# A chunked delta rule on one core: slots reordered, key copies ahead of the norms, one key projection ahead of the states

## The chip, the cores and the metric

The kernel runs on one core of one Trainium2 chip. The metric is the device time of one execution in microseconds. A core has five engines that each run their own list of instructions in order and meet only at semaphores: TensorE (PE; its weight loads are shown as PEld), VectorE (DVE), ScalarE (ACT), GpSimd (POOL) and SyncE (SP), which here starts transfers.

## What is computed

The kernel is a chain of four attention layers and four feed-forward layers. The change touches the fourth attention layer alone, a gated delta rule with 32 heads of 64 channels on two sequences of 1024 tokens of 256 features. Cut to what matters:

```python
qkvz = x @ w_qkvz.T; ba = x @ w_ba.T                  # x: the normalised activations
q, k, v = causal_conv(q, k, v, conv_w)                # 4 taps a channel
g = -exp(A_log) * softplus(a + dt_bias); beta = sigmoid(b)
q = l2norm(q) * DK ** -0.5; k = l2norm(k)
def step(S, (q_t, k_t, v_t, g_t, b_t)):               # over the tokens
    S = S * exp(g_t)
    delta = (v_t - einsum('bhk,bhkv->bhv', k_t, S)) * b_t
    S = S + k_t[..., :, None] * delta[..., None, :]
    return S, einsum('bhk,bhkv->bhv', q_t, S)
o = o * rsqrt(mean(o * o) + EPS) * norm_weight * sigmoid(z)
return o @ w_out.T                                    # added to the residual
```

The kernel does it in chunks of 64 tokens: inside a chunk the recurrence becomes the inverse of a unit lower triangular matrix of 64 x 64 and a few products, and a state of 64 x 64 is handed from chunk to chunk, 16 chunks for a sequence.

## The kernel before

**Units.** Two heads are done together, one in partitions 0 to 63 and one in 64 to 127. A pair of heads and a batch make a unit; there are 16 pairs and 2 batches, so 32 units. `run` calls `step(t, u, f, p)` once a unit on every engine, with four units in flight: `p` (u + 2) is projected and convolved, `f` (u + 1) has its decays, key products and inverse made, `u` runs its states, and `t` (u - 1) is normalised, gated and projected out. Two steps form the body of a hardware loop.

**TensorE** gives the order. `key_side` (L2647): `turn_keys` transposes the keys of f into the PSUM banks B3 and B3+1; `decay` makes the decay exponents in A3, A3+1; `values_and_keys` (L2476) makes u's w and u parts in groups of 8 chunks, `key_products` (L2548) f's products of keys with keys and queries into A3 or B3, `key_sums` (L2664) the matrices of u's states, `decay_upto` (L2541) the decays of the queries. Then `states` (L2700): a chain over 16 chunks. `across(c)` (L2790, L2794) needs state c, which VectorE writes (L3147 for the first, L3149 for the others); `within(c + 1)` (L2768, L2776) does not. After each chunk `beside(c)` puts one piece of other work into the slot: projections `project(p, 0..5)` (L2495), `mean_square` (L2557), the gate's `project_z` (L2504), the output `project_out(t, 0..3)` (L2565, halves by `out_part`), `turn_values` (L2513, the line of both turns), and from slot 9 on the block inverse of f, in products of 32 x 32 (`inverse_y` in slot 9 to `inverse_above` in slot 14, all L2483). `hold` is a wait with an instruction of its own.

**VectorE**, one queue: `convolve` (L3010, nine a unit: kind and tap), `keys` (L3018 to L3026: the sum of squares of the keys, its reciprocal, the two scaled copies of the keys out of B3), `decayed` and `decayed_pairs` (L3040, L3046: products times decays), the sums pT (L3143), then the loop over the states q = 0 to 14 with pieces behind each: `diagonals`, `gather` (L3054, L3061: the diagonal blocks for GpSimd), `decayed_queries` (L3069), `gate` (L3080), `add` (L3087, the residual), `scatter` (L3074, the solved blocks back), `values` (L3032), `masked`, `refined`, `below`, `above` (L3092 to L3107).

**ScalarE**: the squares of the keys (L2852), the exponentials of the decays (L2868, L2874), `outputs` (L2987, L2988: o and its squares out of C3), `parts` (L2936, L2937: w and u out of D3 and C3), the matrices mT (L2950), `compacted` (L2888: three quarters of the blocks to invert), `projected` (L2841, L2842), logs and roots.

**GpSimd**: `scaled` (L2375, decays times beta), `squares` (L2412), `gated` (L2420), then `solve`: the fourth quarter of the blocks (L2384), a copy of the unit blocks (L2387) and the forward substitution, 15 pairs of a product (L2395) and a difference (L2396), each on up to 64 columns and each after the one before; `sided` (L2428, L2429) shapes the result for `scatter`; `gates` and `spread` follow.

**SyncE** loads weights by the counts of projections that TensorE has done.

## Time and profile before

| what | us |
|---|---|
| median of three runs | 4861.91 |
| lowest, highest of them | 4851.96, 4862.69 |
| the profiled execution | 4822.35 |
| its span, first to last instruction | 4820.6 |
| TensorE busy in the span | 4109.9 (85%) |
| VectorE | 2341.0 (49%) |
| ScalarE | 1668.1 (35%) |
| GpSimd | 1264.3 (26%) |

Busy time is the time in which an engine has an instruction of the program at work. The profile is one execution; a statement on an instruction's length comes from it, a statement on the time of the kernel from the runs. The delta rule's 32 steps lie between 2798 and 4594 us of the span, a good third of the kernel. In the timeline a row gives start and length in microseconds, engine, line, operation, result and operands, their form and how many; in square brackets stands how long the engine was idle before and what ended that.

### The profile page before, as it was taken

The page shows a single profiled execution, that of the slowest core. Times are in us where ns is not written, and L with a number is a line of the kernel's source. Part 1 is how long each engine was busy: PE and PEld are TensorE (multiplying, and loading weights), DVE is VectorE, ACT ScalarE, POOL GpSimd, SP SyncE.
Part 4 walks back from the last instruction along what each step waited for, and adds up shares of the span by engine and source line. Part 5 has one row for each costly group of instructions (what it writes and reads, how often), then busy time and mean ns, then how long its engine had stood idle before and what let it go on. Part 6 is the DMA issues. An engine that isn't in the chain of part 4 may idle for free. (4 is left out here: it accounts for less than half of the span.)

```text
span 4820.6 us, 107874 instructions
## 1 busy us (share of the span) xinstructions
PE 4109.9 (85%) x45061; PEld 2478.0 (51%) x45120; DVE 2341.0 (49%) x4073; ACT 1668.1 (35%) x2600; POOL 1264.3 (26%) x1755
## 2 busy tenths in 40 slices
PE   6789759999967859779899589989999889899869
PEld 3333645555534634446556355555555555555546
DVE  5942244545453251440332456666666666666541
ACT  2057122111220113231110345555555555555432
POOL 2000110000015241210000244454455554444412
PEclk9689769999978977889899789998999999889889
DMA  1000000000021510000100000000000000000000
GB/s 46 1 1 1 28 24 1 10 10 7 4 94 56 177 58 0 0 22 1 53 1 1 14 8 9 8 8 8 8 8 8 8 8 8 8 8 8 5 15 18
DMA packets 37930, 91.58 MB, mean 19 GB/s; under 512 B 6993, under 2 KB 27252, under 8 KB 33999
## 3 DMA queue, kind: packets, MB, share of 16 engines
q1 hardware_dynamic: 27150, 69.45, 4.2%
q0 software_dynamic: 6144, 11.62, 0.8%
q8 instruction: 359, 5.88, 0.5%
q10 hardware_dynamic: 4224, 4.19, 0.3%
q14 instruction: 53, 0.43, 0.0%
HBM read 69.96 MB, written 20.45 MB: 19 GB/s over the span
## 5 line engine op out<-in xcount | busy, mean ns | idle before, releaser
L2495 PE MATMUL ps<-h_normT,h_w 128*128 128x512 f32 (+1 forms) x1008 | 476.5, 582 | 76.9 <-DVE h_xx L3074 70.3
L3010 DVE SCALAR_TENSOR_TENSOR h_cv<-h_raw,h_cw,h_cv 128x1023 f32<-128x1023 f32 (+2 forms) x288 | 369.7, 1293 | 20.7 <-ACT h_cv L2842 18.7
L3149 DVE SCALAR_TENSOR_TENSOR h_st<-h_st,d_gcs,ps 128x64 f32<-128x64 f32 x448 | 123.6, 276 | 442.7 <-PE ps L2790 442.2
L2841 ACT ACTIVATE h_raw<-ps 128x512 f32<-128x512 f32 x192 | 114.1, 594 | 469.1 <-PE ps L2495 468.2
L2495 PEld LDWEIGHTS ps<-h_normT,h_w 128*128 128x128 f32 x1008 | 180.9, 211 | 170.8 <-issue 150.1
L2396 POOL TENSOR_TENSOR h_gm<-h_gm,h_tmp 128x15 f32<-128x15 f32 (+7 forms) x480 | 255.3, 532 | 37.6
L837 PE MATMUL ps<-a_probT,a_v 128*128 128x512 f32 x512 | 227.6, 603 | 0.8 <-DVE a_probT L975 0.8
L2395 POOL TENSOR_TENSOR h_tmp<-h_gm 128x15 f32<-128x15 f32 (+7 forms) x480 | 188.9, 394 | 96.5 <-DVE h_gm L3061 61.4
L1960 PE MATMUL ps<-h_normT,e_wgu 128*128 128x512 f32 (+1 forms) x448 | 204.1, 599 | 2.3 <-DMA e_wd<-in_e_wd 1.1
L2790 PEld LDWEIGHTS ps<-h_st,h_mT 64*64 64x64 f32 x1792 | 93.1, 139 | 213.7 <-issue 209.1
L2404 POOL TENSOR_TENSOR h_xT<-h_xx,d_const 32x512 f32<-32x512 f32 x64 | 66.2, 1034 | 487.6 <-DVE h_xx L3097 485.2
L1124 POOL MEMSET r_zero<- 128x2048 f32 x1 | 1.8, 1804 | 727.9 <-POOLq L54 727.9
L2565 PE MATMUL ps<-h_wo,h_o 128*128 128x256 f32 x512 | 172.7, 456 | 5.5 <-DVE h_o L3080 4.7
L407 ACT ACTIVATE a_prob<-ps 128x1024 f32<-128x1024 f32 (+1 forms) x192 | 153.8, 810 | 57.3 <-PE ps L335 19.1
L448 DVE TENSOR_REDUCE a_mx<-ps 128x2 f32<-128x1024 f32 (+2 forms) x192 | 169.2, 952 | 1.9 <-PE ps L296 1.0
L932 ACT ACTIVATE a_prob<-ps,a_nbias 128x1024 f32<-128x1024 f32 x64 | 71.3, 1113 | 284.6 <-DVE a_nbias L985 284.6
L2794 PE MATMUL ps<-h_pT,h_st 64*64 64x64 f32 x1920 | 165.4, 251 | 0.6 <-DVE h_st L3149 0.6
L837 PEld LDWEIGHTS ps<-a_probT,a_v 128*128 128x128 f32 x512 | 98.7, 194 | 124.8 <-issue 123.6
L2790 PE MATMUL ps<-h_st,h_mT 64*64 64x64 f32 x1792 | 154.8, 251 | 6.5 <-DVE h_st L3149 5.6
L148 PE MATMUL ps<-ident,h_norm 128*128 128x128 f32 x256 | 45.3, 360 | 134.7 <-DVE h_norm L127 134.7
L975 DVE COPY a_probT<-ps 128x512 f32<-128x512 f32 x128 | 82.6, 685 | 155.2 <-PE ps L887 155.2
L2548 PE MATMUL ps<-h_cv 64*64 64x128 f32 x2048 | 82.2, 293 | 77.9 <-DVE h_norm L3026 76.6
(537 smaller groups left out, 9492.1 us busy)
## 6 DMA issues: line engine op xcount, KB each, us to landing
m_wgu<-in_m_wgu SPq DMA_DIRECT2D x8, 1408.0 KB
h_w<-in_d_w SPq DMA_DIRECT2D x48, 128.0 KB, 2.2
m_wd<-in_m_wd SPq DMA_DIRECT2D x8, 704.0 KB
m_rows_in<-r_zero SPq DMA_DIRECT2D x4, 1024.0 KB, 14.1
e_xe<-m_rows_in SPq DMA_DIRECT2D x8, 512.0 KB
m_rows_out<-e_y ACTq DMA_DIRECT2D x8, 512.0 KB, 11.2
e_wgu<-in_e_wgu SPq DMA_DIRECT2D x1, 3520.0 KB
a_t_raw<-in_t_w SPq DMA_DIRECT2D x4, 768.0 KB
```

The source lines that it names most:

```text
L407: act.activation(prob[:, u % 3, :, c0:BANK], ps[:, 2 * (u % 3):2 * (u % 3) + 2, c0:BANK], ACT.Exp, scale=1.0 / float(np.sqrt(D0))).then_in ...
L448: dve.tensor_reduce(mx[:, b * NQ + qt, part, m:m + 5:4], ps[:, 2 * (n % 3):2 * (n % 3) + 2, 0:w], AX.X, ALU.max).then_inc(mx_ready, 1)
L837: last = pe.matmul(ps[:, 6 + m, :], v[:, b * NQ + kt, m * P:(m + 1) * P], probT[:, blk % 2, kt, :], start=(kt == 0), stop=(kt == NQ - 1))
L1960: last = pe.matmul(ps[0:m, 3 * (n % 2) + s, :], wgu[:, k, s, c * P:c * P + m], hT[:, k, tok], start=(k == 0), stop=(k == KC - 1))
L2395: c.link(pool.tensor_tensor(part, column, row, ALU.mult))
L2396: c.link(pool.tensor_tensor(target, target, part, ALU.subtract))
L2495: last = pe.matmul(ps[:, PROJ[m], lo:hi], w[:, kind, k, :], hT[:, k, b * S + tb * BANK + lo:b * S + tb * BANK + hi], start=(k == 0), stop= ...
L2565: last = pe.matmul(ps[:, POUT[k], j * H:(j + 1) * H], o[:, tile * P:(tile + 1) * P], wo[:], start=True, stop=True)
L2790: last = pe.matmul(ps[rows(h), D3 + c % 2, 0:HALF], mT[rows(h), c, :], st[rows(h), c, :], start=False, stop=True, tile_position=(64 * h, 6 ...
L2794: last = pe.matmul(res(h, c), st[rows(h), c, :], pT[rows(h), c, :], start=False, stop=True, tile_position=(64 * h, 64 * (1 - h)))
L3010: dve.scalar_tensor_tensor(out=d, in0=raw[:, kind, 0:S - back], scalar=tap(pr, kind, TAPS3 - 1 - back), in1=d, op0=ALU.mult, op1=ALU.add). ...
L3149: last = dve.scalar_tensor_tensor(out=st[:, q + 1, :], in0=st[:, q, :], scalar=scal(gcs, pr, b)[:, q:q + 1], in1=ps[:, D3 + q % 2, 0:HALF] ...
```

## The change

It moves work; no product is added or taken away.

- **Keys.** VectorE makes the copies with `eg` first and in two halves, before the sum of squares; ScalarE's square of the keys is in two halves, in turn with them over the two banks. The copy with `kds` comes last, and `k_ev` counts all three; `kd_d` goes.
- **Order of TensorE in `key_side`.** `key_products(f, 1)` goes behind `values_and_keys(1)`; the wait for the residual's last addition goes from the start to `decay`.
- **One projection ahead.** `project(p, 0)` leaves slot 0 and stands before the states, behind `decay_upto`. The later pieces move up a slot or more: mean square 2 -> 1, gate projection 3 -> 2 and 7 -> 6, projections 4, 5 -> 3, 4, output projections 6, 10, 12, 13 -> 5, 7, 10, and 12 and 13 by halves.
- **Copies.** ScalarE's `outputs` goes ahead of and between the squares of the keys and the decays; `compacted` goes between the two copies of mT.
- **GpSimd.** The fourth quarter (`last_quarter`) goes from behind `gated` to ahead of it.
- **VectorE.** `convolve(f, 6)` goes from before `keys` to between the two `decayed`; `diagonals` and `gather` from behind the first state copy to ahead of it; `decayed_queries`, the other convolutions, `gate` and `add` move up; `below` goes from slot 13 to slot 14; `convolve(p, 5)` goes from the end of the step to slot 12, `add(t, 3)` to the end.

```diff
-        POUT = (B3 + 1, A3, A3, B3)
+        POUT = (B3 + 1, B3 + 1, A3, A3)
...
+            def last_quarter(f, t=None):
+                n = f[0]
+                pool.wait_ge(sqa, 2 * t[0] + 2) if t else pool.wait_ge(db_d, 2 * n + 2)
+                pool.wait_ge(nt_d, 2 * n + 2)
+                pool.tensor_tensor(y[quarter(3), :, :], nT[quarter(3), :, side(3)], one(3), ALU.mult).then_inc(nc3_d, 1)
+                pool.wait_ge(nc3_d, n + 1)
...
                 if t:
                     squares(t)
+                if f:
+                    last_quarter(f, t)
+                if t:
                     gated(t)
                 if f:
-                    solve(f, t)
+                    solve(f)
...
             def key_side(t, u, f, p):
...
-                if t:
-                    hold(xa, 4 * n)
                 if f:
                     hold(ev, 6 * f[0] + 6)
                     hold(x_d, 2 * n + 2)
                     turn_keys(f)
                     hold(y4_d, 2 * n + 2)
+                    if t:
+                        hold(xa, 4 * n)
                     decay(f)
...
-                if f:
-                    hold(k_ev, f[0] + 1)
-                    key_products(f, 1)
                 if t:
                     hold(sqo_d, 2 * n)
                 values_and_keys(1)
+                if f:
+                    hold(k_ev, 3 * f[0] + 3)
+                    key_products(f, 1)
                 key_sums(0)
                 key_sums(1)
                 if f:
                     pe.wait_ge(at_d, 2 * f[0] + 1)
                     decay_upto(f)
+                if p:
+                    pe.wait_ge(at_d, 2 * f[0] + 2)
+                    project(p, 0)
...
                     if c == 0 and p:
-                        pe.wait_ge(at_d, 2 * f[0] + 2)
-                        project(p, 0)
-                    if c == 1 and p:
                         project(p, 1)
-                    if c == 2 and t:
+                    if c == 1 and t:
...
-                    if c == 3:
+                    if c == 2:
...
-                    if c == 7:
+                    if c == 6:
                         pe.wait_ge(zv, 2 * n + 1)
                         project_z(u, 1)
+                    if c == 7 and t:
+                        pe.wait_ge(xa, 4 * n + 1)
+                        project_out(t, 1)
...
                     if c == 10 and t:
                         pe.wait_ge(v_ev, f[0] + 1) if f else pe.wait_ge(lnd, 2 * t[0] + 2)
-                        project_out(t, 1)
+                        project_out(t, 2)
...
                         if f:
-                            inverse_zt(f, (lambda k: out_part(t, 2, k)) if t else None)
+                            inverse_zt(f, (lambda k: out_part(t, 3, 0) if k == 0 else None) if t else None)
...
                         if t:
-                            pe.wait_ge(ev, 6 * p[0] + 6) if p else pe.wait_ge(zv, 2 * n + 2)
-                            project_out(t, 3)
+                            out_part(t, 3, 1)
...
             def key_squares(f):
                 n = f[0]
-                act.wait_ge(trk, n + 1)
-                act.activation(flat(ksq[:]), ps[:, B3:B3 + 2, :].rearrange("p a n -> p (a n)"), ACT.Square).then_inc(ksq_d, 1)
+                for a in range(2):
+                    act.wait_ge(k_ev, 3 * n + 1) if a else act.wait_ge(trk, n + 1)
+                    act.activation(flat(ksq[:])[:, half(a)], ps[:, B3 + a, :], ACT.Square).then_inc(ksq_d, 1)
...
+                if t:
+                    outputs(t, 0)
                 if f:
                     key_squares(f)
+                if t:
+                    outputs(t, 1)
+                if f:
                     decays(f)
-                if t:
-                    outputs(t)
                 parts(0)
                 parts(1)
...
                 for g in range(2):
+                    if f and g == 1:
+                        compacted(f)
                     act.wait_ge(wk, 2 * n + g + 1)
...
-                dve.wait_ge(ksq_d, n + 1)
+                for a in (1, 0):
+                    dve.wait_ge(trk, n + 1) if a else dve.wait_ge(ksq_d, 2 * n + 1)
+                    dve.tensor_tensor(parted(vk[:, b, :, 1, :])[:, a], turned(B3)[:, a], by_parity(scal(eg, pr, b))[:, a], ALU.mult).then_inc(k_ev, 1)
+                dve.wait_ge(ksq_d, 2 * n + 2)
...
-                dve.tensor_tensor(parted(ka[b][:, :, 0, :]), turned(B3), by_parity(kds[:]), ALU.mult).then_inc(kd_d, 1)
-                dve.tensor_tensor(parted(vk[:, b, :, 1, :]), turned(B3), by_parity(scal(eg, pr, b)), ALU.mult).then_inc(k_ev, 1)
+                dve.tensor_tensor(parted(ka[b][:, :, 0, :]), turned(B3), by_parity(kds[:]), ALU.mult).then_inc(k_ev, 1)
...
                 if f:
-                    convolve(f, 6)
                     keys(f)
                     decayed(f, 0)
                     decayed_pairs(f, 0)
+                    convolve(f, 6)
                     decayed(f, 1)
                     decayed_pairs(f, 1)
...
+                if f:
+                    diagonals(f)
+                    gather(f)
                 for q in range(NC3 - 1):
...
                     if f and q == 0:
-                        diagonals(f)
-                        gather(f)
-                    if f and q == 1:
                         decayed_queries(f)
-                    if f and q in (2, 3):
-                        convolve(f, q + 5)
-                    if t and q == 5:
-                        gate(t, 0)
-                    if t and q == 7:
+                    if f and q in (1, 2):
+                        convolve(f, q + 6)
+                    if t and q in (4, 5):
+                        gate(t, q - 4)
+                    if t and q == 6:
                         add(t, 0)
+                    if t and q == 8:
+                        add(t, 1)
...
                     if t and q == 11:
-                        add(t, 1)
-                        gate(t, 1)
+                        add(t, 2)
...
-                    if f and q == 13:
+                    if f and q == 14:
                         below(f)
-                    if t and q in (13, 14):
-                        add(t, q - 11)
-                    if p and q in (4, 6, 7, 10, 12):
-                        convolve(p, (4, 6, 7, 10, 12).index(q))
+                    if p and q in (3, 5, 6, 9, 10, 12):
+                        convolve(p, (3, 5, 6, 9, 10, 12).index(q))
                 if f:
                     above(f)
-                if p:
-                    convolve(p, 5)
+                if t:
+                    add(t, 3)
```

## Rows read from the trace of the kernel before

**Rows 1.** The page: TensorE's granted clock in 40 equal slices, in tenths.

```profile
PEclk9689769999978977889899789998999999889889
```

**Rows 2.** Busy time by windows, all 29 full steps (the first line names the columns).

```profile
core 0: us, PE busy (x) PEld busy (x) DVE busy (x) ACT busy (x) POOL busy (x), PEclk, DMA share, GB/s
2858.17:4542.18 1684.01, 1517.99 (x31357) 968.97 (x31378) 1058.95 (x1596) 884.98 (x1393) 839.48 (x1277) 0.92 0.03 8
```

**Rows 3.** The same by windows, state copy to scatter: one of 29, and their sum.

```profile
3379.81:3399.76 19.95, 18.86 (x248) 9.20 (x240) 12.64 (x20) 15.72 (x24) 15.73 (x33) 1.00 0.01 2
...
sum 578.43, PE 547.17 PEld 266.94 DVE 368.76 ACT 455.89 POOL 456.00; mean PE 18.87 PEld 9.20 DVE 12.72 ACT 15.72 POOL 15.72
```

**Rows 4.** The same by windows, scatter to key squares: three of 29, and their sum.

```profile
3051.16:3070.87 19.71, 18.41 (x620) 13.33 (x621) 13.40 (x21) 6.06 (x9) 5.07 (x5) 1.00 0.02 4
...
3399.76:3422.10 22.34, 20.28 (x620) 14.30 (x622) 14.37 (x22) 6.06 (x9) 5.08 (x5) 0.92 0.01 3
...
4268.02:4293.56 25.54, 23.15 (x620) 15.94 (x622) 14.40 (x22) 6.06 (x9) 5.08 (x5) 0.80 0.02 8
...
sum 675.60, PE 626.23 PEld 438.64 DVE 403.59 ACT 175.81 POOL 147.13; mean PE 21.59 PEld 15.13 DVE 13.92 ACT 6.06 POOL 5.07
```

**Rows 5.** The same by windows, key squares to state copy: one of 29, and their sum.

```profile
3422.10:3435.46 13.36, 11.04 (x221) 8.28 (x220) 9.02 (x14) 8.72 (x16) 8.15 (x8) 1.00 0.01 2
...
sum 429.97, PE 344.58 PEld 263.39 DVE 286.60 ACT 253.28 POOL 236.34; mean PE 11.88 PEld 9.08 DVE 9.88 ACT 8.73 POOL 8.15
```

**Rows 6.** Waits in the loop: us in total, times, longest; the last from 2860 to 4467.

```profile
PE ps L2548 <- DVE h_norm L3026: 70.9, 29, 3.3
PE ps L2495 <- DVE h_xx L3074: 66.5, 29, 2.6
...
PE ps L2513 <- issue: 8.1, 12, 1.2
```

**Rows 7.** Timeline of TensorE at slot 9.

```profile
3400.96 0.67 PE L2495 MATMUL ps<-h_normT,h_w 128*128 128x256 f32 x2 [2.29 <-DVE h_xx L3074]
```

**Rows 8.** Timeline of the key stretch, all engines.

```profile
3422.10 1.02 ACT L2852 ACTIVATE h_mT<-ps 128x1024 f32<-128x1024 f32 x1 [1.82 <-PE ps L2513]
...
3423.16 1.22 DVE L3018 TENSOR_REDUCE h_ssr<-h_mT 128x16 f32<-128x1024 f32 x1 [0.26 <-ACT h_mT L2852]
3423.42 1.80 PE L2476 MATMUL ps<-h_norm,h_xT 64*64 64x128 f32 x30
...
3424.97 0.33 PE L2548 MATMUL ps<-h_cv 64*64 64x128 f32 x2
...
3425.53 1.23 DVE L3025 TENSOR_TENSOR h_ka<-ps,h_kds 128x1024 f32<-128x1024 f32 x1
...
3428.03 1.10 PE L2548 MATMUL ps<-h_cv 64*64 64x128 f32 x32 [1.82 <-DVE h_norm L3026]
...
3433.17 1.98 PE L2541 MATMUL ps<-h_gm,d_const 128*128 128x512 f32 x4
...
3433.92 1.93 ACT L2888 ACTIVATE h_y<-h_nT 32x512 f32<-32x512 f32 x3
```

**Rows 9.** Timeline of GpSimd and VectorE beside it.

```profile
3427.38 2.50 POOL L2412 TENSOR_TENSOR h_sq<-h_sq,h_qsq 128x512 f32<-128x512 f32 x2
...
3437.71 0.22 POOL L2395 TENSOR_TENSOR h_tmp<-h_gm 128x15 f32<-128x15 f32 x1 [1.80 <-DVE h_gm L3061]
...
3440.42 1.28 DVE L3010 SCALAR_TENSOR_TENSOR h_cv<-h_raw,h_cw,h_cv 128x1022 f32<-128x1022 f32 x1
3440.62 1.22 POOL L2396 TENSOR_TENSOR h_gm<-h_gm,h_tmp 128x48 f32<-128x48 f32 x1
...
3447.46 0.75 POOL L2395 TENSOR_TENSOR h_tmp<-h_gm 128x60 f32<-128x60 f32 x1
```

**Rows 10.** Timeline of slot 13.

```profile
3417.01 1.13 PE L2565 MATMUL ps<-h_wo,h_o 128*128 128x256 f32 x4
3417.12 0.70 DVE L3102 TENSOR_SCALAR h_y<-ps 32x512 f32<-32x512 f32 x1 [0.53 <-PE ps L2483]
```

More of the change, by code:

```diff
@@ L2438, in start @@
                 scaled(f)
+                last_quarter(f)
                 solve(f)
@@ L2626, in start @@
                 key_products(f, 0)
-                hold(k_ev, 1)
+                hold(k_ev, 3)
                 key_products(f, 1)
@@ L2645, in start, with key_side @@
                 inverse_above(f)
-            def key_side(t, u, f):
+            def key_side(t, u, f, p):
                 n, pr, b = u
@@ L2718, in beside @@
                         project_z(u, 0)
-                    if c in (4, 5) and p:
+                    if c in (3, 4) and p:
                         if t:
-                            pe.wait_ge(lnd, 2 * t[0] + c - 3)
+                            pe.wait_ge(lnd, 2 * t[0] + c - 2)
                         else:
                             pe.wait_ge(egx, 2 * f[0] + 2)
-                        project(p, c - 2)
-                    if c == 6 and t:
+                        project(p, c - 1)
+                    if c == 5 and t:
                         if p:
@@ L2951, in step @@
                 if f:
-                    compacted(f)
                     decays_upto(f)
```

40 lines of the change are left out of this document (18 added, 22 removed).

## Prediction, made before the changed kernel was built or run

> **What bounds the kernel now.** I read the page's slices first: the changed code fills slices 24 to 38 of 40, and there TensorE's granted clock (full is 2.4 GHz, half 1.2) never stays full for long [rows 1]. So I cut the loop into its 29 full steps with the table by windows. They last 1684.0 us, 58.07 us a step, at a mean granted clock of 0.92 [rows 2]. Each step falls into three stretches, by instructions that occur once a step: the first state copy (VectorE, L3147), the first transpose that scatters the solved blocks (VectorE, L3074) and the squares of the keys (ScalarE, L2852).
>
> State copy to scatter lasts 19.95 us in 28 of 29 steps, whatever else varies: sum 578.4 us [rows 3]. A stretch so constant follows one chain: GpSimd's forward substitution (L2395, L2396), to which nothing is given between its first and last instruction. Scatter to key squares: 19.71 us at best, 23.30 us in the mean (675.6 / 29); 27 of 29 are below clock 1.00, and the length goes with the clock: 19.71 at 1.00, 22.34 at 0.92, 25.54 at 0.80 [rows 4]. Key squares to state copy: 13.36 us in the step at 3422 (13.16 at best), 14.83 in the mean (430.0 / 29) [rows 5]; 15 of 29 are below 1.00.
>
> The table of waits names what TensorE lacks: 66.5 us before L2495 for the scatter, 70.9 us before L2548 for VectorE's copy of the keys, each once a step [rows 6]. The timeline shows the order around the first: TensorE has come to the block inverse, stands 2.29 us, and starts 1.20 us after the scatter did (3399.76) [rows 3, 7]. The second is 1.82 us in the step at 3422 [rows 8]. So neither TensorE nor another engine is full: a step is a ring, key squares -> decays -> substitution -> scatter -> inverse -> next key squares, and the clock falls behind the wait in it.
>
> **Key stretch, new order.** Zero is the start of the key squares; rows of the step at 3422 [rows 8]. The copies of the keys no longer wait for the norms: VectorE takes half the bank pair (512 columns, 0.70 us, as L3102 has it [rows 10]), ScalarE squares one half while VectorE copies the other, so the last square ends at 1.4 instead of 1.02. From the reduce's start to the scaled copy L3025 is 2.37 us (3423.16 to 3425.53), and that copy takes 1.23: k_ev reaches its third count at 5.05. Before, L3026 behind it ended at 5.8.
> TensorE: the first value-and-key group starts at 1.32, and 1.55 us later (3423.42 to 3424.97) key_products(0) wants the decays. ScalarE now has two halves of squares, one output pair and two decays ahead of that: 0.8 + 4 x 0.48 + 0.6 = 3.3 (starts of its 512-column copies lie 0.48 apart). **New wait: 0.45.** Then 1.1 (L2548) + 1.55 + 1.1 + 2 x 1.1 (L2664): 9.3. k_ev at 5.05 and the w and u copies are long there, so the waits of 1.82 and 0.39 go. Then decay_upto 1.91 (L2541, 1.98 with its last overlap) and the moved project(p, 0), again 1.91: the states start at 13.1, against 13.0 before (3433.17 + 1.91). The projection is no new work: slot 0 loses it.
> VectorE: nT(0) 4.97, its pair 5.57, then convolve(f, 6), which used to stand before the reduce. Queued behind it are nT(1), and behind that compacted, the last key-sum copy, pT(1), the diagonals, and now also the first state copy, which everybody waits for. It takes 1.28 us if it runs freely (L3010 [rows 9]). The bounds of its price are 1.28 and 1.28 + 1.25, as GpSimd is at its squares (L2412, two in 2.50) then; I take 0.6 of waiting, half of one such instruction, since it meets it midway. nT(1) ends at 8.75, compacted (L2888, 1.93) at 10.7, mT(1) 11.3, pT(1) 11.9, transpose 1.08 and gather 0.48: 13.45. GpSimd: from bep at 3.3 the 8.15 us that it is busy in this stretch [rows 5], 1.28 blocked by the convolution, and 0.6 for the copy of the unit blocks (L2387): 13.3. Behind gated, in its old place, last_quarter would hold up the transpose; where it is put, both queues end together. Substitution starts at 13.9 (bounds 13.4 and 14.9), against 15.61 before (3437.71).
>
> **Substitution.** Start of L2395 to scatter: 17.70 us (3437.71 to 3435.46 + 19.95) [rows 3, 5, 9]. The rows show what lengthens it: L2396 of 48 columns takes 1.22 us while VectorE's convolution runs, 0.3 us otherwise, and a product takes 0.75 beside gate [rows 9]. Inside it remain the decayed queries and five convolutions; gate(t, 1), so far in slot 11, joins. gate(0) costs 0.45 (0.75 - 0.30). Sum 17.70 + 0.45 = 18.15 (bounds 17.9 and 18.9); **scatter at 32.05** after the squares, against 34.78 in the mean (14.83 + 19.95) and 33.3 at best.
> The Trainium skill ("SBUF — State Buffer", section "SBUF: two separate sides") says that a VectorE instruction with two SBUF inputs and a GpSimd instruction hold one port pair as an exclusive lock, for the whole instruction. By these rows the trace agrees in kind (1.22 for 0.3), with a loss a little below the instruction's own length. By the page gate(1) would cost its whole 0.75: an estimate of 0.30 more a step, 9 us in all. The rule speaks against putting convolve(f, 6) beside GpSimd's squares.
> TensorE between state start and slot 9: 19.3 us before (3400.96 - 2.29, less 3379.81 - 0.4 [rows 3, 7]), now minus a projection (1.98) plus an output projection (1.13): 18.45, so it arrives at 31.55 and can go on 1.20 after the scatter, at 33.25: **the wait shrinks from 2.29 to 1.7** and is then for GpSimd alone.
> The stacked slots of VectorE: slot 5 has gate 0.75 and a convolution 1.28 beside a TensorE slot of only 1.13, so state 6 comes some 0.9 late; slot 6 (1.98 of gate projection) covers it. project_out(1) in slot 7 waits for add(0), ready 0.5 before. ScalarE's norms end 8.7 after the state start (two table loads of 1.28 among them), gate(0) asks at 9.9: covered by 1.2; were that cover gone, the state chain itself would wait.
>
> **Inverse stretch.** Slots 12 and 13 lose one output projection, 1.13 (two halves of 0.56) [rows 10]; below(f) moves from slot 13 to slot 14, behind state 14. Before, it began 3417.12, beside a projection, and nobody waited. Now state 14 comes with TensorE's next step, below takes 0.70 more, and inverse_above is queued behind it: TensorE arrives 1.05 early. Bounds 0.5 and 1.4. So 19.71 - 1.13 + 1.05 = 19.65: the saved projection is given back. I add 0.3 for TensorE's own issue gaps in turn_keys (8.1 us in 28 steps [rows 6]). convolve(p, 5) goes into slot 12, where another convolution stood, and at the end add(3) is done before decay asks for it. Both convolutions that stood between the end of a step and the reduce of the keys, 2.5 us, are gone from there, so an early turn_keys no longer finds VectorE occupied.
>
> **Sum at full clock:** 32.05 + 19.65 + 0.3 = 52.0. **Clock:** in the old inverse stretch the slow part costs 23.30 - 20.0 = 3.3 a step. It stands behind a wait of 2.3. A wait of 1.82 in the key stretch was followed by a stretch at 1.00 [rows 5, 8], but two rows of the inverse stretch at 1.00 out of 29 say that there the fall is easy. At 1.7 I expect it in six of ten, 2.0 us a step; in the key stretch, left with 0.45 and 0.16 of waiting, none. Bounds 0 and 3.3. **Step 54.0 us, gain 4.07, 30 steps: 122 us.** The profiled execution took 4822.35 us (span 4820.6), so 4700 of its own kind; the median of the three runs is 4861.91, 39.6 above, which I keep: 4740 us.
>
> **Rivals.**
> 1. The clock stays up behind the shorter wait: 52.0 a step, 30 x 6.07 = 182, 4680 us. For it: key waits of 1.82 at 1.00. Against: the little matrix products around the inverse.
> 2. The clock falls as often as before: 55.3, 30 x 2.77 = 83, 4779 us. For it: 27 of 29.
> 3. VectorE's one queue becomes the bound: convolve(f, 6) loses a full 1.25 and diagonals, now ahead of the state copy, wait for GpSimd's last_quarter behind squares. Scatter at 34.8 as before; 34.8 + 19.95 + 2.0 = 56.7, gain 41, 4821 us; slightly worse and it is no change. For it: the sums of both queues end within 0.2 of each other.
> 4. Slower: the new 1.05 wait between inverse_below and inverse_above falls into the stretch where nearly all products are 32 or 64 wide, and a second fall of the clock follows there. The stretch took 5.8 us more at a clock of 0.80 than at 1.00 (25.54 against 19.71 [rows 4]), and 5.8 is what this has to cost before it decides: a mean clock of 0.80 in every step, where the first fall alone gives some 0.85. At 0.75 (7.3 us by the same rate) the step is 52.0 + 0.2 + 7.3 = 59.5, 30 x 1.43 = 43 more, 4905 us. Against it: 1.05 is well below the 1.82 behind which no fall came.
> 5. The order of TensorE does not do what it says: project(p, 0) before the states waits for at_d(2), 9.4 by my sum, needed at 11.2. If it were late the states would start late, but GpSimd would not: price near 0, part of the range.
>
> **Chances.** Forecast 0.44, rival 1 0.19, rival 2 0.20, rival 3 0.12, rival 4 0.04, an unseen wait of no net effect 0.01. The range takes the forecast and rivals 1 and 2 with their bounds: 4675 to 4812. A measurement here can tell about 0.3% (15 us) from no change. Faster by more than that: 0.91 (all of the first three, most of rival 3); within it 0.05; slower 0.04.
>
> **What would show it.** Wait before L2495 in slot 9 between 1.2 and 2.0 us; no wait before L2548 for VectorE, instead some 0.45 for ScalarE's decays; a wait near 1 us before inverse_above; state copy to scatter again constant but about 18.5; key stretch about 13.5 without exception; the inverse stretch between 19.9 and 23 by its clock. If state copy to scatter is not constant, GpSimd no longer binds and the sum is wrong; if squares to state copy exceeds 14.5, VectorE's queue is rival 3.

## The result: faster by about 1.1%, less than half of what was forecast

| | before | changed |
|---|---|---|
| median of four runs, us | 4862.3 | 4809.26 |
| lowest to highest | 4851.96 to 4879.81 | 4803.58 to 4823.99 |
| profiled execution, us | 4822.35 | 4812.68 |
| mean granted clock in the span | 0.886 | 0.875 |

The ratio is 0.989, with a 95% interval of 0.986 to 0.993: 53 us less. The time lies just inside the range, and the sign was right; the size was not: 122 us were forecast. A second set of runs of the same changed kernel on another chip gave 0.987 (0.985 to 0.989).

The two profiled executions must not be subtracted. The loop of the changed kernel starts 53.5 us later in its profile, at 2852.0 instead of 2798.5, though all that the device does before is the same code. The jump is made in the mixture-of-experts stage, which the change does not touch: its additions L1269 begin 66.6 us later. In the profile of the second set the loop starts at 2803.6. This goes with the chip: on the two on which the kernel before took 4827.41 and 4833.87 us, the loop starts at 2798.9 to 2812.7 in all eight profiles, on the one on which it took 4858.59, at 2844.4 to 2852.1 in all three. The profile of before has the short stage beside a median of the long kind, which would explain most of the 39.6 us by which it lay below it. What makes the stage longer is open. These are the first state copy and the additions of the changed kernel, by the view of one line (durations min, median, max in ns; first and last start in us):

```profile
L3167 DVE COPY h_st<-ps x32: 210/218/225, 2852.0 to 4583.3; 128x64 f32<-128x64 f32 x32
```
```profile
L1269 DVE SCALAR_TENSOR_TENSOR x_resid<-ps,m_sgate,x_resid x8: 474/480/484, 1553.8 to 1589.5; 128x256 f32<-128x256 f32 x8
```

and the same of before:

```profile
L3147 DVE COPY h_st<-ps x32: 224/224/226, 2798.5 to 4593.3; 128x64 f32<-128x64 f32 x32
```
```profile
L1269 DVE SCALAR_TENSOR_TENSOR x_resid<-ps,m_sgate,x_resid x8: 476/480/485, 1487.2 to 1527.9; 128x256 f32<-128x256 f32 x8
```

What compares is the step of the loop. Busy time by windows of the changed kernel, first all 29 full steps, then the sums over its three stretches (state copy to scatter, scatter to key squares, key squares to state copy), to be read beside [rows 2 to 5]:

```profile
2911.21:4535.59 1624.38, 1505.57 (x31373) 967.91 (x31371) 1053.91 (x1625) 890.67 (x1422) 871.37 (x1276) 0.91 0.03 8
```
```profile
sum 530.32, PE 503.16 PEld 255.45 DVE 354.11 ACT 380.06 POOL 453.16; mean PE 17.35 PEld 8.81 DVE 12.21 ACT 13.11 POOL 15.63
```
```profile
sum 674.94, PE 589.31 PEld 428.43 DVE 364.38 ACT 203.32 POOL 147.34; mean PE 20.32 PEld 14.77 DVE 12.56 ACT 7.01 POOL 5.08
```
```profile
sum 419.12, PE 413.10 PEld 284.02 DVE 335.42 ACT 307.30 POOL 270.87; mean PE 14.24 PEld 9.79 DVE 11.57 ACT 10.60 POOL 9.34
```

| us a step | before | changed | forecast |
|---|---|---|---|
| state copy to scatter | 19.95 | 18.29 | 18.5 |
| scatter to key squares | 23.30 | 23.27 | 21.95 |
| key squares to state copy | 14.83 | 14.45 | 13.5 |
| sum | 58.07 | 56.01 | 54.0 |

2.06 us a step are 62 us over 30 steps; the medians show 53. The waits of TensorE in these 29 steps (us in total, times, longest) answer to [rows 6]:

```profile
PE ps L2503 <- DVE h_xx L3091: 61.9, 29, 2.5
PE ps L2491 <- DVE h_y L3119: 34.4, 29, 1.5
PE ps L2491 <- issue: 7.8, 15, 0.9
PE ps L2521 <- issue: 5.1, 8, 1.0
PE ps L2778 <- DVE h_pT L3160: 4.1, 5, 1.7
```

The wait for the keys' copies, 70.9 us, is gone altogether, as forecast. The new wait for ScalarE's decays, forecast at 0.45 a step, did not come (0.2 us in all 29 steps). The one for the scatter in slot 9 is hardly shorter (61.9 against 66.5), and there is the new one of 1.19 us before `inverse_above` in slot 14. TensorE's idle time fell, but its clock stayed as low: 0.91 in the loop, 0.92 before [rows 2]. A fall is a place in the trace's clock record where the granted clock goes from full to half. The falls can be counted by where they begin: behind slot 9's wait (within 8 us of the start of the scatter), around slot 14 (from there to the key squares; in none of the traces does one begin between 8 and 14 us after the scatter), or in the key stretch. Before there were 27, 1 and 14 falls in 29 steps; now there are 14, 26 and 0. Those around slot 14 begin between 0.1 us before and 3.2 us after the start of the wait there. Half clock holds for 9.65 us a step against 8.95. Two windows of the step at 4164, on either side of the wait in slot 14, show it (columns as in [rows 2]; the clock is the last but two):

```profile
4163.95:4181.14 17.19, 14.79 (x484) 10.29 (x485) 11.14 (x17) 5.48 (x8) 4.96 (x5) 1.00 0.04 11
4181.14:4188.00 6.86, 6.86 (x172) 5.44 (x174) 4.35 (x7) 4.53 (x9) 0.12 (x1) 0.75 0.02 5
```

Up to the wait the clock is full, with the wait in slot 9 (2.07 us) inside it; behind it, full and half alternate. The timeline of that place, and of the key stretch behind it:

```profile
4179.99 0.28 DVE L3169 SCALAR_TENSOR_TENSOR h_st<-h_st,d_gcs,ps 128x64 f32<-128x64 f32 x1 [1.03 <-PE ps L2800]
4180.30 0.70 DVE L3119 TENSOR_SCALAR h_y<-ps 32x512 f32<-32x512 f32 x1
4181.14 1.47 PE L2491 MATMUL ps<-h_xx,h_y 32*32 32x32 f32 x64 [1.20 <-DVE h_y L3119]
```
```profile
4188.34 2.04 POOL L2375 TENSOR_TENSOR h_dec<-h_dec,h_bep 128x512 f32<-128x512 f32 x2 [7.08 <-DVE h_bep L3040]
4188.38 1.03 DVE L3042 TENSOR_TENSOR h_kds<-h_bep,d_egr 128x16 f32<-128x16 f32 x1
4189.45 1.22 DVE L3043 TENSOR_TENSOR h_ka<-ps,h_kds 128x1024 f32<-128x1024 f32 x1
4190.34 2.52 POOL L2416 TENSOR_TENSOR h_sq<-h_sq,h_qsq 128x512 f32<-128x512 f32 x2
...
4191.78 2.15 DVE L3025 SCALAR_TENSOR_TENSOR h_cv<-h_raw,h_cw,h_cv 128x1023 f32<-128x1023 f32 x1
...
4199.50 0.67 POOL L2399 TENSOR_TENSOR h_tmp<-h_gm 128x15 f32<-128x15 f32 x1 [0.56 <-DVE h_gm L3078]
```

Two of VectorE's instructions are long in this step: `kds`, 16 columns, takes 1.03 us beside GpSimd's first product of `scaled`, and `convolve(f, 6)` 2.15 us beside GpSimd's squares. The step is not typical in the first: `kds` took 1.03 in only 4 of the 29 steps (5 in the second profile of this kernel) and 0.18 in the others, and in the kernel before in 14 of 29. The median and the longest of all 32, changed and before:

```profile
L3042 DVE TENSOR_TENSOR h_kds<-h_bep,d_egr x32: 174/176/1032, 2790.8 to 4524.7; 128x16 f32<-128x16 f32 x32
```
```profile
L3024 DVE TENSOR_TENSOR h_kds<-h_bep,d_egr x32: 174/177/1031, 2737.0 to 4532.0; 128x16 f32<-128x16 f32 x32
```

The convolution took 1.78 in the mean. The substitution starts at 4199.50, 14.7 us after the key squares (4184.78), as in the mean of the 29 steps (14.68). Forecast was 13.9; the kernel before had 15.6 in the one step that the forecast was read from, and 17.06 in the mean.

### The profile page after: what moved, and what is told of

It reads as the page before. It is cut to its first block and busy times, and to the rows that moved or that the text cites. A ratio compares the mean times of both kernels' runs of the same rounds, so it can differ in the third digit from the quotient of the medians.

```text
span 4811.0 us, 108050 instructions
## 1 busy us (share of the span) xinstructions
PE 4129.2 (86%) x45120; PEld 2489.1 (52%) x45120; DVE 2334.5 (49%) x4105; ACT 1675.6 (35%) x2632; POOL 1298.3 (27%) x1755
## 5 line engine op out<-in xcount | busy, mean ns | idle before, releaser
L2503 PE MATMUL ps<-h_normT,h_w 128*128 128x512 f32 (+1 forms) x1008 | 451.8, 555 | 73.1 <-DVE h_xx L3091 66.3
L3025 DVE SCALAR_TENSOR_TENSOR h_cv<-h_raw,h_cw,h_cv 128x1023 f32<-128x1023 f32 (+2 forms) x288 | 384.9, 1337 | 19.7 <-ACT h_cv L2852 18.6
L2399 POOL TENSOR_TENSOR h_tmp<-h_gm 128x15 f32<-128x15 f32 (+7 forms) x480 | 252.4, 526 | 65.4 <-DVE h_gm L3078 30.3
L2400 POOL TENSOR_TENSOR h_gm<-h_gm,h_tmp 128x15 f32<-128x15 f32 (+7 forms) x480 | 202.5, 422 | 37.6
L2491 PE MATMUL ps<-h_xx,h_y 32*32 32x32 f32 x6144 | 125.6, 205 | 37.7 <-DVE h_y L3119 37.3
```

What stands on the lines that cost most here:

```text
L2399: c.link(pool.tensor_tensor(part, column, row, ALU.mult))
L2400: c.link(pool.tensor_tensor(target, target, part, ALU.subtract))
L2491: last = pe.matmul(ps[quarter(to), n, c * DB2:(c + 1) * DB2], lhsT(r, c), rhs(r, c), start=True, stop=True, tile_position=(32 * r, 32 * to))
L2503: last = pe.matmul(ps[:, PROJ[m], lo:hi], w[:, kind, k, :], hT[:, k, b * S + tb * BANK + lo:b * S + tb * BANK + hi], start=(k == 0), stop= ...
L3025: dve.scalar_tensor_tensor(out=d, in0=raw[:, kind, 0:S - back], scalar=tap(pr, kind, TAPS3 - 1 - back), in1=d, op0=ALU.mult, op1=ALU.add). ...
```

## Theories, and the experiments that tell them apart

Theory A: the wait that `below(f)` causes in slot 14 gives back the saved time, once by itself and once through the falls of the clock behind it; the falls come from waits. Rival B: they come from products that are 32 and 64 wide. Beside these: GpSimd's and VectorE's common port makes the start of the substitution late. The ratios below are to the kernel before on the same chip, with 95% intervals; a step of the loop is the mean over 29 steps in the profile. As said, totals of two chips differ by some 30 to 50 us from elsewhere; ratios hardly, and the step by 0.3 us in the two profiles of the changed kernel (56.01 and 55.72).

### One detail undone: below behind state 13

```diff
-                    if f and q == 14:
+                    if f and q == 13:
                         below(f)
```

> The changed kernel with one part undone: VectorE's copy below(f) stands behind state 13 again, not behind state 14. Theory A: TensorE's new wait of 1.20 us before inverse_above is what lets its clock fall in the last slots (26 of 29 steps). Then both the wait and the falls behind it go: 1.2 us and about 2 us of half clock a step, 30 x 3.2 = 96, some 4713 us; the inverse stretch, scatter to key squares, falls from 23.3 to about 20.5 us in the mean, and wherever no fall stands behind slot 9 its clock is 1.00. Rival B: the clock falls there because the products are only 32 and 64 wide, whatever the wait. Then 1.2 us a step go alone, 36 in all, some 4773 us, and the falls stay.

Measured: 4710.05 us, ratio 0.975 (0.971 to 0.979), against 0.987 to 0.989 with the change as made. The step is 54.49 us: 18.31, 22.03, 14.16. Its sum over the inverse stretch, and its waits, which no longer name L3119:

```profile
sum 638.90, PE 567.93 PEld 406.33 DVE 364.89 ACT 202.75 POOL 147.41; mean PE 19.58 PEld 14.01 DVE 12.58 ACT 6.99 POOL 5.08
```
```profile
PE ps L2503 <- DVE h_xx L3091: 63.9, 29, 2.5
PE ps L2491 <- issue: 16.0, 28, 1.3
PE ps L2521 <- issue: 13.9, 12, 1.8
PE ps L2778 <- DVE h_pT L3160: 7.0, 11, 1.7
```

Falls: 15 behind slot 9, 10 around slot 14 instead of 26; half clock for 5.65 us a step instead of 9.65. The total is near theory A's 4713, but both expectations started from 4809, and the kernel before is 28 us shorter on this chip. Counted in ratios, the detail is worth 1.2 to 1.5% (against 0.987 and against 0.989), 59 to 71 us, where rival B gave 36 and theory A 96. By the step it is 1.2 to 1.5 us (against 55.72 and against 56.01), 37 to 46 in all, where A gave 3.2; the profiled execution, 4723.18 us, was the longest of the four, 13 above the median. So by the ratio it is more than the wait's own length, as A has it, by the step hardly more, and in both well below A's size. That the clock gains is plain from its count; what it gave was partly lost again: the idle time that the profile puts to TensorE's own issue grew from 0.45 to 1.03 us a step (perhaps because the wait had covered it; that is not shown), and the inverse stretch reached 22.0, not 20.5.

### That detail alone, in the kernel before

```diff
-                    if f and q == 13:
+                    if f and q == 14:
                         below(f)
```

> The kernel before with that one part alone: below(f) behind state 14. Theory A: a wait of about 1 us arises before inverse_above and the clock falls behind it in most steps: 1.0 + 1.5 us a step, 30 x 2.5 = 75, some 4937 us; the inverse stretch goes from 23.3 to 25.8 us. Rival B: only the wait, 30 us, some 4893. Rival C: in the kernel before, additions of the residual stand behind state 13, so that state 14 comes later and the wait is larger, up to 1.7 us, without more falls: 4913.

Measured: 4860.67 us, ratio 1.007 (1.005 to 1.009). The step is 58.85 us, 0.78 more. The wait is there, 1.20 us each time, and the wait for the keys' copies shrinks from 2.45 to 1.79, since VectorE gets on while TensorE stands:

```profile
PE ps L2495 <- DVE h_xx L3074: 66.7, 29, 2.6
PE ps L2548 <- DVE h_norm L3026: 51.9, 23, 3.4
PE ps L2483 <- DVE h_y L3102: 34.8, 29, 1.4
```

Falls: 25, 11 and 10, half clock 9.3 us a step against 8.95. So the same wait of 1.20 us brings 10 falls around slot 14 here (11 instead of 1), and 4 fewer in the key stretch. In the changed kernel it brings 13 to 16 (26 and 23 with it, 10 without), and 10 stand there with no such wait at all: the detail explains the larger part of the 26, and something else in the new order the rest. Rival B's sum (4893 against a before of 4862, that is +31) is the nearer one; against the kernel before on this chip 27 us were measured. Theory A in its simple form, a wait of 1.2 us lets the clock fall, does not hold here: what stands around the wait counts too. The changed kernel has half an output projection less in each of slots 12 and 13; whether that is the something else is open.

### GpSimd released by kds

```diff
-                dve.tensor_tensor(bep[:], rec[:], scal(beta, pr, b), ALU.mult).then_inc(bep_d, 1)
-                dve.wait_ge(bep_d, n + 1)
-                c.link(dve.tensor_tensor(kds[:], bep[:], scal(egr, pr, b), ALU.mult))
+                c.link(dve.tensor_tensor(bep[:], rec[:], scal(beta, pr, b), ALU.mult))
+                dve.tensor_tensor(kds[:], bep[:], scal(egr, pr, b), ALU.mult).then_inc(bep_d, 1)
+                dve.wait_ge(bep_d, n + 1)
```

> The changed kernel, with GpSimd released by the product kds (L3042 there) instead of by the one before it (bep). In the profile of the changed kernel kds, on 16 columns, takes 1.03 us while GpSimd's first product of scaled runs, where it took 0.17 before. Theory: the two want the same port pair and VectorE waits for GpSimd's instruction. Then kds is back at 0.17, GpSimd starts 0.3 later, the scaled copy of the keys 0.85 earlier, and the substitution 0.3 to 0.8 earlier: 30 x 0.5 = 15, some 4794 us. Rival: kds is long for another reason (the wait for bep) and stays near 1 us; then the kernel gets 0.3 us a step slower or stays at 4809.

Measured: 4757.59 us, ratio 0.987 (0.982 to 0.992): no difference from the changed kernel that the runs can show. The profile shows the cause of the 1.03 us, though:

```profile
4126.72 0.18 DVE L3041 TENSOR_TENSOR h_kds<-h_bep,d_egr 128x16 f32<-128x16 f32 x1
4126.94 1.22 DVE L3043 TENSOR_TENSOR h_ka<-ps,h_kds 128x1024 f32<-128x1024 f32 x1
4126.98 2.04 POOL L2375 TENSOR_TENSOR h_dec<-h_dec,h_bep 128x512 f32<-128x512 f32 x2 [7.66 <-DVE h_kds L3041]
4128.98 3.49 POOL L2416 TENSOR_TENSOR h_sq<-h_sq,h_qsq 128x512 f32<-128x512 f32 x2
4129.33 2.00 DVE L3025 SCALAR_TENSOR_TENSOR h_cv<-h_raw,h_cw,h_cv 128x1023 f32<-128x1023 f32 x1
```

With GpSimd not yet at work it takes 0.18, in every step of this profile. The Trainium skill ("SBUF — State Buffer", section "SBUF: two separate sides") states an exclusive lock for a whole instruction, in both directions. The trace agrees: in the changed kernel `kds` is held for 0.85 us by a GpSimd product of 1.04, and in the rows above the convolution (2.00 instead of 1.28) and the squares (3.49 instead of 2.50) hold each other. The key stretch became 14.20 us instead of 14.45 and 14.31. There was little to gain: `kds` was long in 4 or 5 of 29 steps, in the mean 0.12 to 0.15 us a step over its 0.17.

### convolve(f, 6) behind both decayed_pairs

```diff
-                    convolve(f, 6)
                     decayed(f, 1)
                     decayed_pairs(f, 1)
+                    convolve(f, 6)
```

> The changed kernel, with convolve(f, 6) behind both decayed and both decayed_pairs instead of between them. In the profile it takes 2.15 us beside GpSimd's squares, and nT(1), compacted, pT(1), the diagonals and the first state copy are queued behind it. Theory: that queue sets when the substitution starts. Then the first state copy comes about 1.0 us earlier after the key squares (13.5 instead of 14.5), the wait before slot 9's inverse falls from 2.1 to about 1.1 us and the clock falls less often behind it: 1.0 to 2.5 us a step, 4734 to 4779. Rival: behind them it meets GpSimd's last quarter and holds that up instead, as much as it gave: 4809, state copy at 14.5.

Measured: 4763.07 us, ratio 0.985 (0.980 to 0.989), intervals overlapping with the change as made. The key stretch is 14.37 us in the mean, 13.4 at best, the wait in slot 9 2.02. Falls around slot 14 (26) reach into the key stretch. Its length goes with that: 13.4 to 13.7 in the nine steps with at most 1.3 us of half clock in it, 14.1 to 15.9 in the other twenty. In one of these, the step at 3971, VectorE waits 1.33 us for TensorE's second key products. The expected 1.0 us did not come; whether it would without those falls, the run with three details asks.

### Below, kds and the convolution together

> The changed kernel with three of its details the other way: below(f) behind state 13, GpSimd released by kds, convolve(f, 6) behind both decayed_pairs. Below behind state 13 alone had 0.975. If GpSimd's and VectorE's common port sets the start of the substitution, the state copy comes 13.4 to 13.6 us after the key squares instead of 14.2, which falls in slot 14 hid when the convolution was moved alone; slot 9's wait shrinks to 1.3 to 1.6 us and fewer falls stand behind it: 1 to 2 us a step more than below alone, ratio 0.963 to 0.969. Rival: the decays or TensorE's own order set it, the state copy stays at 14.2 and the ratio at 0.975.

Measured: 4703.02 us, ratio 0.975 (0.973 to 0.976); the step is 54.05 us: 18.40, 21.71, 13.94. The key stretch is 0.2 shorter than with below alone (14.16), the wait in slot 9 is 2.27, not shorter. The rival is the right one: the two small delays of VectorE's queue are worth 0.4 us a step at most and nothing that the totals show. My forecast's term for the convolution was small, and it is not what was missing.

### The changed kernel again, and project(p, 0) back in slot 0

> The changed kernel again, unchanged, beside the next three on the same chip, so that they can be compared with it directly. Both theories expect the ratio to the kernel before that it had, 0.989 (0.986 to 0.993), and the same picture: a wait of about 2.1 us in slot 9, one of 1.20 in slot 14, falls of the clock behind the first in some 18 of 29 steps and behind the second in some 22.

Measured: 4759.94 us, ratio 0.987 (0.985 to 0.989), step 55.72 us, falls 15, 23 and 0.

```diff
-                if p:
-                    pe.wait_ge(at_d, 2 * f[0] + 2)
-                    project(p, 0)
                 hold(mt_d, 2 * n + 2)
...
                     if c == 0 and p:
+                        pe.wait_ge(at_d, 2 * f[0] + 2)
+                        project(p, 0)
                         project(p, 1)
```

> The changed kernel with the projection of the keys, project(p, 0), back in slot 0 (together with project(p, 1)) instead of before the states. Theory: it is a move inside the stretch that GpSimd's queue sets; TensorE has the same work between the key squares and slot 9, and waits before the states (2.5 us for pT instead of 0.1 to 0.6) for what it had as work. The state copy comes when the diagonals are gathered, as before: ratio 0.989, slot 9's wait unchanged at 2.1 us. Rival: the long wait before the states lets the clock fall in the key stretch, as it did in the kernel before (14 of 29 steps), but that part is not bound by TensorE: at most 0.5 us a step, ratio 0.992. Second rival, the projection ahead is what made the change work: without it the key stretch is 1.9 us longer and the ratio 1.00.

Measured: 4741.40 us, ratio 0.981 (0.980 to 0.983): **faster than the changed kernel on the same chip**, by 0.5%, which none of the three expected. The step is 54.93 us. The waits:

```profile
PE ps L2777 <- DVE h_pT L3159: 45.0, 29, 2.4
PE ps L2491 <- DVE h_y L3118: 34.0, 29, 1.5
PE ps L2503 <- DVE h_xx L3090: 20.8, 27, 1.1
```

From key squares to slot 9 TensorE waits as long as before, 2.27 us a step; but it is 1.55 before the states and 0.72 in slot 9, instead of 0.16 and 2.13. Falls: 0, 26 and 3 instead of 15, 23 and 0; half clock 6.2 us a step instead of 8.6. Behind a wait of 0.25 to 1.07 us in slot 9 not one fall is left; the 3 in the key stretch begin 13.4 to 14.1 us after the key squares, at the new wait before the states. The projection ahead of the states is no gain: it gathers TensorE's wait in one place, slot 9, and the clock falls there.

### Both, below behind state 13 and project(p, 0) in slot 0

> The changed kernel with two details undone: below(f) behind state 13 and project(p, 0) in slot 0. The second alone gave 0.981 where the changed kernel has 0.987 on the same chip, the first alone 0.975. Theory: TensorE waits 2.3 us in all between the key squares and the inverse; one wait of 2.1 lets the clock fall more often than two of 1.5 and 0.7. Then the gains add up: ratio 0.969, with about 1.5 us before the states and 0.7 in slot 9, and falls after slot 9 in some 8 steps. Rival: once the wait in slot 14 is gone, the split brings little: 0.973 to 0.975.

Measured: 4739.33 us, ratio 0.976 (0.972 to 0.979), against a kernel before of 4858.59 on this chip. By the step it is 53.69 us, the lowest without a filled slot 9 (below alone 54.49): 19.03, 20.57, 14.09. Falls: 0 behind slot 9, 13 around slot 14 (one of them 0.1 us into the key squares), and 8 within 1.4 us before to 0.2 us after the state copy, at the wait of 1.7 us before the states; half clock 3.3 us a step. The interval does not tell this ratio from that with below alone (0.971 to 0.979); by the step the gain of the split is 0.8 us, as it was alone (55.72 to 54.93). State copy to scatter is no longer constant (18.33 to 20.93; 18.33 to 20.92 with the projection alone): the half clock of these last falls reaches into the states.

### The wait in slot 9 filled

```diff
             def inverse_y(f, beside=None):
+                if beside:
+                    for part in range(4):
+                        beside(part)
                 hold(xd_d, 2 * f[0] + 1)
                 for part in range(4):
-                    if beside:
-                        beside(part)
                     some = range(GC4 * part, GC4 * (part + 1))
```

In the kernel with three details:

> The kernel of the last run, and the four pieces of project(p, 4), so far laid between the four parts of inverse_y behind its wait for the scatter, put ahead of that wait. Work of 2.0 us then fills a wait of 1.5 to 2.1 us in slot 9. Theory A, the clock falls behind waits: wait and falls go, 1.5 to 2.0 plus about 1.3 us a step, ratio 0.945 to 0.952. Rival B, the clock falls in the block inverse because its products are 32 wide: they now stand in one piece of 1.6 us, the falls stay or increase: 1.5 to 2 us alone, ratio 0.955 to 0.96. Rival C: slot 9's wait was no loss, since what follows waits for ScalarE's copies of that projection: no change against the last run.

Measured: 4661.46 us, ratio 0.967 (0.965 to 0.969). The step is 52.37 us: 18.42, 20.07, 13.88. The whole loop, and what TensorE waits for:

```profile
2863.01:4381.61 1518.60, 1412.51 (x31345) 932.89 (x31372) 1057.81 (x1625) 887.48 (x1422) 877.41 (x1276) 0.97 0.03 9
```
```profile
PE ps L2491 <- issue: 28.5, 35, 2.4
...
PE ps L2491 <- DVE h_xx L3092: 10.4, 23, 0.6
```

The wait fell from 2.27 to 0.36 a step, the falls from 15, 8 and 0 to 6, 6 and 2, the clock is 0.97. Against rival B: the products of `inverse_y` now stand in one piece, 128 products with nothing wide among them, and the clock falls less. But 1.68 us a step were gained, not 3.3, and 39 us for the whole, 0.8%, is less than either theory gave. Part of the rest is a new stop: in 10 of the 29 steps TensorE stands for 1.7 to 2.4 us, until some 5 us after the scatter, and the profile names nothing that it waits for ("issue"). With it the inverse stretch takes 21.9 us in the mean, without it 19.1; all 6 falls that are left behind slot 9 are in steps with it, and two of them last 24 us.

In the kernel before, alone:

> The kernel before, with nothing of the change, and the four pieces of project(p, 4) put ahead of the wait for the scatter in slot 9. Theory A, the falls of the clock in the inverse stretch come from that wait of 2.29 us: the wait shrinks to 0.3, the falls behind slot 9 from 27 of 29 steps to fewer than 10: 2.0 + 2.1 us a step, loop 54.0 us a step, ratio 0.975. Rival B, they come from products that are 32 wide: 2.0 us a step, the falls stay, ratio 0.988. The wait for the keys' copies and the falls in the key stretch (14 of 29) stay by either.

Measured: 4762.18 us, ratio 0.980 (0.978 to 0.982), step 54.95 us: 19.96, 20.39, 14.60. This one edit brings nearly twice what the whole change brought (0.989). Its sum over the inverse stretch, beside 675.60 in [rows 4]:

```profile
sum 591.30, PE 537.51 PEld 396.55 DVE 403.11 ACT 175.99 POOL 147.38; mean PE 18.53 PEld 13.67 DVE 13.90 ACT 6.07 POOL 5.08
```
```profile
PE ps L2548 <- DVE h_norm L3027: 66.4, 29, 3.4
PE ps L2483 <- issue: 11.1, 12, 2.6
PE ps L2665 <- ACT h_u L2938: 11.0, 29, 0.4
PE ps L2483 <- DVE h_xx L3075: 10.7, 28, 0.4
```

Falls: 8 behind slot 9 instead of 27, in the key stretch 12 instead of 14. For slot 9 this is clear: in the same kernel, with the same products, the falls went with the wait. Wait and falls together are worth 2.91 us a step in the stretch, where the filled time is 2.0. The mean hides two kinds of steps. In 21 of 29 the stretch takes 18.55 us with 0.16 us of half clock in it. In the other 8 the same kind of stop stands, 2.0 to 2.7 us, with one fall beside each, and the stretch takes 25.2; four of these falls last 24 to 27 us. Two neighbouring steps by windows (the clock is the last but two), and the end of such a stop in another, 5.1 us after its scatter:

```profile
3086.53:3116.11 29.58, 26.62 (x617) 19.25 (x616) 14.19 (x22) 6.07 (x9) 5.08 (x5) 0.58 0.01 3
3149.43:3167.60 18.17, 16.66 (x617) 12.46 (x616) 13.39 (x21) 6.07 (x9) 5.08 (x5) 1.00 0.04 12
```
```profile
3527.53 0.21 PE L2795 MATMUL ps<-h_pT,h_st 64*64 64x64 f32 x1 [2.09 <-issue]
```

The kernels without a filled slot 9 have no stop of this length there. What makes it is open. The steps with it lengthen the stretch's mean by 1.84 us.

And with project(p, 0) in slot 0 on top of the kernel of 0.967:

> The kernel with four details changed (0.967) and project(p, 0) in slot 0 as well. Slot 9's wait is filled there (0.4 us), so there is nothing to split: TensorE gets a wait before the states of about 1.5 us and is late by as much in slot 9, or it catches up in the slots. Theory: ratio 0.967 to 0.972, the state copy to scatter at 18.4, the inverse stretch at 20 to 21 us. Rival: the state chain starts 1.9 us earlier and that is worth something by itself: below 0.964.

Measured: 4704.08 us, ratio 0.967 (0.963 to 0.970), step 52.50 us: nothing to split, nothing gained, as the theory had it. The stop stands in 4 of the 29 steps here, 1.5 to 2.6 us.

All profiles side by side; falls in 29 steps behind slot 9, around slot 14, in the key stretch or the states:

| | ratio | us a step | falls | half clock, us a step |
|---|---|---|---|---|
| before | 1 | 58.07 | 27, 1, 14 | 8.95 |
| before, below behind state 14 | 1.007 | 58.85 | 25, 11, 10 | 9.30 |
| before, slot 9 filled | 0.980 | 54.95 | 8, 1, 12 | 5.53 |
| changed | 0.989 | 56.01 | 14, 26, 0 | 9.65 |
| changed again | 0.987 | 55.72 | 15, 23, 0 | 8.59 |
| kds first | 0.987 | 55.95 | 13, 26, 0 | 9.18 |
| convolution behind | 0.985 | 55.96 | 14, 26, 1 | 9.55 |
| below behind state 13 | 0.975 | 54.49 | 15, 10, 0 | 5.65 |
| these three | 0.975 | 54.05 | 15, 8, 0 | 5.18 |
| project(p, 0) in slot 0 | 0.981 | 54.93 | 0, 26, 3 | 6.24 |
| with below behind state 13 | 0.976 | 53.69 | 0, 13, 8 | 3.30 |
| the three, slot 9 filled | 0.967 | 52.37 | 6, 6, 2 | 3.53 |
| the same, project(p, 0) in slot 0 | 0.967 | 52.50 | 3, 8, 0 | 4.00 |

## Why the prediction was right in sign and wrong in size

- **State copy to scatter** ("again constant but about 18.5"): right, 18.29. The length of the substitution from its first product to the scatter was given as 18.15; it is 18.20 in the step at 4185 (4199.50 to 4217.70), 17.9 to 18.2 in 28 of 29.
- **The wait for the copies of the keys goes**: right, to nothing. The 0.45 for ScalarE's decays in its place did not come. The state start, 13.1 us after the key squares, is 13.2 (4197.99 less 4184.78).
- **The start of the substitution, 13.9** (bounds 13.4 to 14.9): 14.7 in the mean, but 13.96 to 13.99 in the five steps with a short `kds` and at most 1.3 us of half clock in the key stretch: as a sum at full clock it was right. In the 20 steps with more half clock it is 14.3 to 15.8. The waiting of the convolution was given as 0.6 and is 0.50 in the mean. A long `kds` is missing in the sum, but it comes in 4 of 29 steps, with a start at 14.6 to 14.7; the lock that I cited for the convolution held for it as well. The run with both removed gained 0.4 us a step over below alone.
- **The wait in slot 9, 1.7**: 2.13. TensorE arrived when forecast (31.76 after the key squares, in the step at 4185; 31.55 in the sum), the scatter came 0.9 late in that step, 0.7 in the mean.
- **The new wait in slot 14, 1.05**: right, 1.19, and so was "the saved projection is given back".
- **The clock behind slot 9, six of ten**: 14 and 15 of 29, about five of ten.
- **The step that failed** is the clock behind slot 14. I priced that wait at its own length, set a fall there into a rival of 0.04, and dismissed it with "1.05 is well below the 1.82 behind which no fall came". In the changed kernel 26 falls in 29 steps stand around it (23 in the second profile), and 10 are left with the wait gone. The 1.82 stood in the key stretch, among products 64 x 128 and 512 columns wide. There it was no accident: in the kernel before, none of the seven waits of 0.50 to 1.82 us in that place had a fall at or behind it, and 14 of the 22 of 1.94 to 3.31 had. But a limit read there was carried to a place with other work around. Rival 4 had the mechanism; what it did not have is that it adds to, and does not replace, the gains elsewhere. With the detail undone the ratio is 0.975, which is 4740 us of 4862, the forecast for the whole. That is luck: the forecast had 1.05 us for the wait, which this run does not have, and in its place stand a key stretch 0.7 us longer than forecast and 5.65 us of half clock where I expected 4; the step is 54.49, not 54.0.
- **Half clock in sum**: I expected about 4 us a step (2.0 of cost); it was 9.65. Of the 2.0 us that the step is longer than forecast, 1.3 are in the inverse stretch and 0.95 in the key stretch, into which falls from slot 14 reach (2.3 us of half clock a step, where I had none), less 0.2 elsewhere.
- **Rival 5** priced a late projection ahead of the states near 0, and no rival asked what the move itself costs. It is a loss of 0.8 us a step: it moves 1.4 us of waiting into the one place where it hurts.
- That the profiled execution lay below the median was kept as a constant of 39.6; it was most likely a long or short stage elsewhere, and did no harm if both medians hold the long one.

Left open: what brings some 10 falls around slot 14 in the changed kernel with no wait for `below`, where the kernel before has 1; what the stop of 2 us is that comes with a filled slot 9; whether products 32 wide make a fall easier behind a wait, as they stand around both places and no run takes them away. And whether the wait for the copies (2.3 us a step, 12 falls) is worth removing once slot 9 is filled was not run alone in that kernel.

## What to carry to other kernels

Here a wait of TensorE could cost its length and the half clock behind it, so the same total waiting was cheaper in two pieces than in one, and cheapest with work that is ready placed ahead of it: moving four pieces of a projection across one wait gained 2.0%, reordering a whole step 1.1%. Before moving a copy one slot later on an engine with idle time, look at who is queued for it: the idle time of VectorE said nothing on the 1.2 us that TensorE then stood. When VectorE and GpSimd both read two operands from SBUF, charge each with the other's instruction, the 16-column ones too, but count in how many steps they meet: one step of a trace showed 0.85 us where the mean was 0.12. Count falls of the clock by their place as well, since a mean of the clock does not tell which wait they stand behind.

## What the runs showed of the hardware

- A VectorE product on 16 columns took 1.03 us when it met a GpSimd product, 0.18 otherwise.
- Around a wait of 1.20 us TensorE's clock fell to half 26 times in 29 steps in one order of work (10 without the wait) and 11 times in another (1 without it). It stayed full behind one of 2.07 us in the step at 4164, and behind all of 0.25 to 1.07 us in slot 9 once `project(p, 0)` was back in slot 0.
- With the wait in slot 9 filled, half clock in that stretch went from 7.21 us a step to 0.16 in 21 of 29 steps; in the other 8 TensorE stopped for 2.0 to 2.7 us with nothing named in the profile, and the clock fell beside every one.
- The loop starts some 40 us later on one chip (three profiles) than on two others (eight), with the same code ahead of it.
